# A transformer layer with top-1 expert routing: gate logits of four tiles at once, experts counted last in a step, half of the tiles stored turned

## The chip, the cores and the metric

The kernel runs on one core of a Trainium2 chip. The core has TensorE (PE, matrix products and transposes into PSUM), VectorE (DVE), ScalarE (ACT), GpSimd (POOL, here small powers, one addition per tile and indirect DMAs), and SyncE (SP), which here only issues DMAs. Each engine works through its own list in order, and semaphores tie the lists together. The metric is the device time of one execution in microseconds; lower is better.

## The reference, cut to what matters

```python
x = x + layernorm(attention(layernorm(x)))        # 2048 tokens of 512; local windows and 64 global queries per head
h = layernorm(x)                                  # 2048 x 512, the input of the gate and the experts
probs = softmax(h @ Wg); eidx = argmax(probs)     # 8 experts, one per token
pos   = running count of the token's expert, over all tokens in order
keep  = pos < 256                                 # each expert takes its first 256 tokens
xd[eidx * 256 + pos] = h                          # dispatch
oe    = (silu(xd @ W1) * (xd @ W3)) @ W2          # per expert, 512 -> 704 -> 512
shared = (silu(h @ sw1) * (h @ sw3)) @ sw2        # for every token
x = x + layernorm(gate * keep * oe[eidx * 256 + pos] + shared)
```

Products are made in about single precision: each operand is split into a rounded part and a rest (`fp32r`), and three products are added (`product3`). The change concerns `h @ Wg`, the running count, and how the second half of `h` is stored for the shared expert.

## The kernel before, in words

Tokens stand in 16 tiles of 128. The kernel has an attention part (until about 410 us), whose last steps already normalise tiles 0 to 3, and then twelve passes of the feed-forward network, held in the list `passes`: passes 0 and 1 are the shared expert on tiles 0 to 3 and 4 to 7, passes 2 to 9 are experts 0 to 7 with 256 rows each, passes 10 and 11 are the shared expert on tiles 8 to 15. A pass has `up` (six blocks m of 128 hidden units, each 24 products for m under 5 and 12 for m = 5, then `step(m)`), and `down` (pairs of output tiles, six blocks each, with `between` after each block). Products of passes 0, 1, 10 and 11 have 512 moving columns, those of the experts' `up` 256.

Beside passes 0 and 1 runs a software pipeline over the tiles, `work()`, one tick n per call: tick 7 ahead of pass 0, ticks 8 to 12 in `step(0)` to `step(4)` of pass 0, ticks 13 to 15 in `between` of its `down`, ticks 16 to 21 in `step(0)` to `step(5)` of pass 1. Tick n does, in this order, `h_logits(n-5)`, `h_turn(n-4)`, `h_h2(n-3)`, `h_mean2(n-2)`, `h_x1(n-1)`, `h_mean(n)`:

- `h_mean`, `h_x1`, `h_mean2` and `h_h2` normalise, add the residual, and write the normalised tile h2 (DVE statistics of L281 and L282, a power on POOL L284, ACT for the tile itself); `h_h2` also stores tiles 8 to 15 in `scr_h2` for passes 10 and 11.
- `h_turn` transposes h2 on PE (four transposes a tile) and copies it out: tiles 0 to 7 as two parts in XT (ACT the first, DVE the rest), the input of passes 0 and 1; tiles 8 to 15 whole in XL, only for the gate.
- `h_logits` multiplies the turned tile with the gate's weights. For tiles 0 to 7 the tile is the stationary operand and the 16 columns of `wghl` (two parts of 8 experts) move: eight products a tile. For tiles 8 to 15 it is four single-precision products, each two entries of the trace.
- After every fourth tile `route_count` finds the expert of each token and adds up counts on DVE (LG, OHB, CUM, CUMB). One tick later `route_place` takes OHB and CUMB as operands of sixteen tiny products on PE (eight times two), makes the row numbers FSI from them on DVE, and POOL scatters the four tiles into `scr_xd`. For the last four tiles it also does the softmax's sum.

Counts of group g run at ticks 8, 12, 16 and 20, right behind the logits of the group's last tile and ahead of the rest of the tick; `route_place` runs at ticks 9, 13, 17 and 21. DVE does in every `step(m)` the product and the rest of block m (SIL, HH), a rest of W2 (W2L), rests of W1 and W3 (W13L), and then the tick.

`prepare` loads the rows of a coming pass and turns them with `turned`, four transposes a tile. Rows for the experts come from `scr_xd`, and their first load waits for the last scatters: it is issued in the `down` of pass 1, and its tiles are turned in `between` at block 4 of the second pair. At the end of pass 1, `next_13` splits seven blocks of the next expert's W1 and W3 on ACT and DVE ahead of `down`, two of them ahead of tick 21 and five behind it.

PSUM banks: UP (four banks, in turn) for `up` and `route_place`, DN for `down`, TPC for transposes, MSC for logits.

Of the kernel before, what the change touches and what calls it, by code (L numbers as in the profile page):

```python
# [5 lines left out]
ALU = mybir.AluOpType  # L6
# [7 lines left out]
P = 128  # L14
# [6 lines left out]
E = 8  # L21
# [84 lines left out]
def sandwich(nc, x, wq, bq, wk, bk, wv, bv, wg, w1, w3, w2, s1, s3, s2, out):  # L106
# [16 lines left out]
    with ExitStack() as top:  # L123
# [56 lines left out]
        wghl = sb(top, "wghl", [P, 4, 2, E], F32R)  # L180
        wt8 = sb(top, "wt8", [P, E])
# [259 lines left out]
        with ExitStack() as st:  # L441
# [165 lines left out]
            def proj_group(g4):  # L607
# [39 lines left out]
                for n in range(2):  # L647
                    for c in range(4):
# [31 lines left out]
                        if n == 1 and c == 3 and g4 == 0:  # L680
                            m_wg.extend(split(wghl[:, :, 0, :], wghl[:, :, 1, :], wgs[:, :, :], "dve", [m_bias]))
                            stores.append(dma("sp", zs, lambda g: g.dma_start(
# [246 lines left out]
        def h_h2(t):  # L929
# [13 lines left out]
            if t >= 8:  # L943
                r0 = (t - 8) * P
                m = dma("sp", h2s[t % 2], lambda g: g.dma_start(h2d[r0:r0 + P, :], dst),
                        [m_h] + h2_marks[-2:-1])
                h2_marks.append(m)
                h2free[t % 8].append(m)

        def h_turn(t):  # L950
# [12 lines left out]
            else:  # L963
# [7 lines left out]
                TPC.busy[ti] += d["s"]  # L971
            h2free[t % 8].append(m_t)
# [311 lines left out]
        with ExitStack() as st:  # L1284
# [109 lines left out]
            scat = []  # L1394
            def h_logits(t):

                g4, j = divmod(t, 4)
                d = hs[t]
                if j == 0:
                    route["mi"], route["mb"], route["mfree"] = MSC.take()  # L1400
                mb, dst = route["mb"], d["dst"]
                if g4 < 2:
                    col = d["col"]
                    for k in range(4):
                        for l in range(2):
                            m_l = mm(mb[:, j * 16:(j + 1) * 16].rearrange("p (l e) -> p l e", l=2),
                                     dst[l][:, k, col:col + P], wghl[:, k, :, :], k == 0 and l == 0,
                                     k == 3 and l == 1, d["s"] + m_wg + route["mfree"], mark=(k == 3 and l == 1))
                    XT.busy[xt[g4]["i"]].append(m_l)
                else:  # L1410
                    for k in range(4):
                        m_l = mm(mb[:, j * 16:j * 16 + E], dst[:, k, :], wgs[:, k, :], k == 0, k == 3,
                                 d["s"] + m_wg + route["mfree"], mark=(k == 3))
                    XL.busy[d["li"]].append(m_l)
                route["m_l"] = m_l

            def route_count(g4):
# [3 lines left out]
                if g4 < 2:  # L1421
# [298 lines left out]
```

How the kernel before makes its waits and increments, by code:

```python
    def emit(self, e, eng):  # L90
        reached = {}
        for after, fn, inc in self.q[e]:
            need = {}
            for m in after:
                if m is not None and m.count > need.get(id(m.sem), (0, None))[0]:
                    need[id(m.sem)] = (m.count, m.sem)
            for key, (count, s) in need.items():
                if count > reached.get(key, 0):
                    eng.wait_ge(s, count)
                    reached[key] = count
            ins = fn(eng)
            if inc is not None:
                ins.then_inc(inc[0], inc[1])
```

## Time and profile before

| | us |
|---|---|
| median of 3 runs | 833.17 |
| lowest, highest | 830.14, 836.89 |
| profiled execution, its own time | 837.23 |
| its span | 835.5 |
| busy: PE, DVE, ACT, POOL | 783.1, 563.4, 423.3, 146.2 |
| mean granted clock of TensorE | 0.982 of full |

The profile is of one execution. Its times are from the first instruction of the span. The duration of a matmul in the trace contains its run through the array; what it takes in a row of matmuls is the distance between starts.

### The profile page before, as it was taken

What the parts mean: (1) busy time and instruction counts of PE and PEld (TensorE: products, weight loads), DVE (VectorE), ACT (ScalarE), POOL (GpSimd) and SP (SyncE); (2) the same over time, 40 slices, a digit from 0 to 9 for tenths busy, and PEclk for the clock granted to TensorE, in tenths of its full rate; (3) what the DMA queues carried; (4) which work ended last, traced back from release to release, by engine and by line L of the source; (5) the groups of instructions that cost most, each with busy time, mean ns of one, the idle gap of its engine ahead of it and who ended that gap; (6) DMA issues with size and microseconds to landing.
All of it is one profiled execution on the core that took longest, in us unless ns stands there. A gap on an engine that the chain in (4) does not pass through costs nothing.

```text
span 835.5 us, 13875 instructions
## 1 busy us (share of the span) xinstructions
PE 783.1 (94%) x5060; PEld 656.0 (79%) x5060; DVE 563.4 (67%) x1196; ACT 423.3 (51%) x839; POOL 146.2 (18%) x227
## 2 busy tenths in 40 slices
PE   4989999989999999999999999999999999999994
PEld 3768878767777777777778887899999999987883
DVE  4654699457888656777578656267766667848666
ACT  3455353525565666676545345466656666723120
POOL 2300010420110211333234631000000000013122
PEclk9989999999999999999999999999999999999998
DMA  6589554974767678873238831656877776546444
GB/s 211 190 248 344 185 175 157 293 205 130 205 161 202 171 201 234 237 214 105 78 102 286 322 127 58 195 175 205 252 215 239 235 223 212 176 164 184 169 152 138
DMA packets 117492, 162.39 MB, mean 194 GB/s; under 512 B 17364, under 2 KB 65236, under 8 KB 117424
## 3 DMA queue, kind: packets, MB, share of 16 engines
q1 hardware_dynamic: 113840, 153.54, 60.5%
q0 software_dynamic: 3584, 7.97, 3.2%
q8 instruction: 40, 0.66, 0.3%
q14 instruction: 28, 0.23, 0.1%
HBM read 107.24 MB, written 55.05 MB: 194 GB/s over the span
## 4 chain that ended last, share of the span: by engine, by line
PE 70%; DVE 15%; issue 5%; ACT 5%; DMA 3%; POOL 1%; POOLq 0%; DVEq 0%
PE bank L163 46%; PE wide L163 18%; PE wide L167 3%; PE bank L167 2%; DVE MX L160 2%; DVE SG L160 1%; ACT PTG L145 1%; ACT PT L157 1%; DMA QSe<-MR 1%; DVE GC L153 1%; DVE STC L281 1%; DMA XX<-scr_xd 1%; DVE TI L747 1%; DVE SIL L149 1%; DVE hl L149 1%
## 5 line engine op out<-in xcount | busy, mean ns | idle before, releaser
L163 PE MATMUL wide<-W2H,HH 128*128 128x512 f32 x308 | 101.9, 397 | 0.5 <-ACT OUTR L145 0.5
L160 DVE TENSOR_REDUCE MX<-wide 128x1 f32<-128x192 f32 (+1 forms) x128 | 77.6, 647 | 25.7 <-PE wide L163 20.2
L157 ACT ACTIVATE PT<-bank 128x512 f32<-128x512 f32 x128 | 73.4, 593 | 29.9 <-PE bank L163 27.7
L157 ACT ACTIVATE SIL<-bank 128x256 f32<-128x256 f32 (+1 forms) x72 | 32.6, 453 | 99.3 <-PE bank L163 99.0
L149 DVE TENSOR_TENSOR SIL<-bank,SIL 128x256 f32<-128x256 f32 (+1 forms) x72 | 36.9, 512 | 65.0 <-ACT SIL L157 64.4
L163 PE MATMUL bank<-XT,W13H 128*128 128x256 f32 (+1 forms) x336 | 76.6, 322 | 0.0
L145 ACT ACTIVATE HH<-SIL 128x256 fp32r<-128x256 f32 (+1 forms) x72 | 35.2, 489 | 67.2 <-DVE SIL L149 67.2
L163 PEld LDWEIGHTS wide<-W2H,HH 128*128 128x128 f32 x308 | 58.6, 190 | 13.2 <-ACT OUTR L145 1.3
L149 DVE TENSOR_TENSOR HH<-SIL,HH 128x256 fp32r<-128x256 f32 (+1 forms) x72 | 37.0, 514 | 45.5 <-ACT HH L145 35.0
L163 PE MATMUL wide<-W2L,HH 128*128 128x512 f32 x168 | 66.4, 395 | 0.8 <-DVE W2L L149 0.8
L163 PEld LDWEIGHTS bank<-XT,W13H 128*128 128x128 f32 x336 | 55.0, 188 | 4.7
L163 PE MATMUL bank<-WQL,W13H 128*128 128x256 f32 (+1 forms) x168 | 55.4, 330 | 0.0
L163 PE MATMUL bank<-WKL,W13H 128*128 128x256 f32 (+1 forms) x168 | 54.4, 324 | 0.0
L163 PE MATMUL bank<-WQL,W13L 128*128 128x256 f32 (+1 forms) x168 | 54.1, 322 | 0.0
L284 POOL TENSOR_TENSOR STC<-STC,mhalf 128x1 f32<-128x1 f32 x48 | 29.0, 604 | 140.5 <-DVE STC L153 135.9
L163 PE MATMUL bank<-XT,W13L 128*128 128x256 f32 (+1 forms) x168 | 53.6, 319 | 0.0
L163 PE MATMUL bank<-WVH,HT 128*128 128x512 f32 x128 | 41.9, 415 | 6.3 <-DVE HT L149 4.7
L163 PE MATMUL bank<-HT,WQH 128*128 128x512 f32 x128 | 42.4, 413 | 3.6 <-DVE HT L149 3.6
L149 DVE TENSOR_TENSOR W13L<-R,W13H 128x512 fp32r<-128x512 f32 x70 | 44.1, 688 | 1.7 <-ACT W13H L145 1.7
L1517 POOL DMA_INDIRECT H2A<-scr_oe,FG x8 | 8.0, 995 | 210.6 <-issue 210.6
L163 PE MATMUL bank<-XT,WQH 128*128 128x256 f32 (+1 forms) x192 | 43.0, 319 | 0.0
L149 DVE TENSOR_TENSOR W2L<-R,W2H 128x512 fp32r<-128x512 f32 x60 | 41.2, 687 | 1.5 <-issue 0.2
(256 smaller groups left out, 2019.0 us busy)
## 6 DMA issues: line engine op xcount, KB each, us to landing
R<-in_L_ffn_W_dram SPq DMA_DIRECT2D x48, 512.0 KB, 5.3
scr_q<-hl SPq DMA_DIRECT2D x16, 512.0 KB, 4.1
scr_k<-hl SPq DMA_DIRECT2D x16, 512.0 KB, 4.2
R<-in_L_ffn_sw_dram SPq DMA_DIRECT2D x12, 512.0 KB, 5.5
QSe<-scr_q SPq DMA_DIRECT2D x36, 128.0 KB, 3.9
KSe<-scr_k SPq DMA_DIRECT2D x36, 128.0 KB
scr_v<-vt SPq DMA_DIRECT2D x16, 272.0 KB, 2.2
R<-_attn_hidden_states_dram SPq DMA_DIRECT2D x16, 256.0 KB, 4.3
```

What stands on the lines that cost most here:

```text
L145: return do(e, lambda g: g.activation(dst, src, ACT.Copy), after)
L149: return do(e, lambda g: g.tensor_tensor(dst, a, b, op), after)
L153: return do(e, lambda g: g.tensor_scalar(dst, a, s1_, None, op0), after)
L157: return do("act", lambda g: g.activation(dst, src, fn, **kw), after)
L160: return do("dve", lambda g: g.tensor_reduce(dst, src, AXX, op), after)
L163: return do("pe", lambda g: g.matmul(ps, a, b, start=start, stop=stop, skip_group_check=True), after, mark=mark)
L167: return do("pe", lambda g: g.transpose(ps, a, idn), after, mark=mark)
L281: a = do("dve", lambda g: g.bn_stats(st[:, 8:14], src), after)
L284: return do("pool", lambda g: g.tensor_tensor(st[:, 2:3], st[:, 3:4], mhalf[:, :], ALU.pow), [a, m_half])
L747: m = do("dve", lambda g: g.max_index(i8, v8, N_[:, :]), prev)
L1517: mg = dma("pool", ga_slots[i], lambda e: e.indirect_dma_start(out=gb, out_offset=None, in_=oed, in_offset=bass.IndirectOffsetOnAxis(ap=FG ...
```

## The change

Gate. For tiles 0 to 3 and 4 to 7 `logits_group` makes the logits of four tiles in eight products: the 16 columns of `wghl` are stationary and 512 token columns of XT move, the result is 16 x 512. ACT copies it out to a buffer of XL, and one call later `logits_fold` turns it back with four single-precision products against `fold`, a 16 x 8 matrix of two identities, which also adds the two parts. `h_logits` remains for tiles 8 to 15. ACT's copy and one addition at the head of `route_count` become one DVE copy.

Order. In ticks 8, 16 and 20 `route_count` runs after everything else of the tick. The count of tiles 4 to 7 moves from tick 12 to `step(5)` of pass 0. `route_place` stays at ticks 9, 13 and 17, and that of the last group moves from `step(5)` of pass 1 to `between` behind the first block of its `down`, which is behind the seven splits of `next_13`.

Storage. Tiles 8 to 15 are stored from XL, turned, one tick later than before; passes 10 and 11 load them and split them from SBUF directly, without transposes.

```diff
--- before.py
+++ after.py
@@ -178,6 +178,7 @@
         onesb = sb(top, "onesb", [P, P], BF16)
         wgs = sb(top, "wgs", [P, 4, E])
         wghl = sb(top, "wghl", [P, 4, 2, E], F32R)
+        fold = sb(top, "fold", [2 * E, E])
         wt8 = sb(top, "wt8", [P, E])
         e256 = sb(top, "e256", [P, E])
         mhalf = sb(top, "mhalf", [P, 1])
@@ -679,6 +680,7 @@
                                 split_w(1, c)
                         if n == 1 and c == 3 and g4 == 0:
                             m_wg.extend(split(wghl[:, :, 0, :], wghl[:, :, 1, :], wgs[:, :, :], "dve", [m_bias]))
+                            m_wg.append(tt(fold[:, :], ident[0:2 * E, 0:E], ident[0:2 * E, E:2 * E], ALU.add, [m_id]))
                             stores.append(dma("sp", zs, lambda g: g.dma_start(
                                 xdd.rearrange("(i p) d -> p i d", p=P),
                                 zt[:, :].unsqueeze(1).broadcast_to([P, 16, D])), [k0]))
@@ -940,13 +942,6 @@
             XX.busy[xi].append(m_h)
             STC.busy[d["si"]].append(m_h)
             d["m_h"] = m_h
-            if t >= 8:
-                r0 = (t - 8) * P
-                m = dma("sp", h2s[t % 2], lambda g: g.dma_start(h2d[r0:r0 + P, :], dst),
-                        [m_h] + h2_marks[-2:-1])
-                h2_marks.append(m)
-                h2free[t % 8].append(m)
-
         def h_turn(t):
 
             g4, j = divmod(t, 4)
@@ -969,6 +964,11 @@
                 d["s"] = [copy("act", d["dst"][:, :, :], tb[:, :].rearrange("p (k t) -> p k t", k=4),
                                [m_t] + fr)]
                 TPC.busy[ti] += d["s"]
+                r0 = (t - 8) * P
+                m = dma("sp", h2s[t % 2], lambda g: g.dma_start(
+                    h2d[r0:r0 + P, :], d["dst"][:, :, :].rearrange("p k t -> p (k t)")), d["s"] + h2_marks[-2:-1])
+                h2_marks.append(m)
+                XL.busy[d["li"]].append(m)
             h2free[t % 8].append(m_t)
 
         with ExitStack() as st:
@@ -1392,37 +1392,47 @@
             route = dict(cum=m_cum)
             scat_slots = [slot() for _ in range(4)]
             scat = []
+            def logits_group(g4):
+
+                ui, ps, fr = UP.take()
+                li, lt, lf = XL.take()
+                x_ = xt[g4]
+                for l in range(2):
+                    for k in range(4):
+                        m_l = mm(ps[0:2 * E, :], wghl[:, k, :, :].rearrange("p l e -> p (l e)"),
+                                 x_["b"][l][:, k, :], k + l == 0, k + l == 4, x_["ready"] + m_wg + fr, mark=(k == 3 and l == 1))
+                XT.busy[x_["i"]].append(m_l)
+                m_c = copy("act", lt[0:2 * E, :, :].rearrange("p k t -> p (k t)"), ps[0:2 * E, :], [m_l] + lf)
+                UP.busy[ui].append(m_c)
+                route["lt"] = (li, lt, m_c)
+
+            def logits_fold():
+
+                li, lt, m_c = route["lt"]
+                route["mi"], route["mb"], fr = MSC.take()
+                for j in range(4):
+                    m_l = mm(route["mb"][:, j * 16:j * 16 + E], lt[0:2 * E, j, :], fold[:, :], True, True,
+                             [m_c] + m_wg + fr, mark=(j == 3))
+                XL.busy[li].append(m_l)
+                route["m_l"] = m_l
+
             def h_logits(t):
 
-                g4, j = divmod(t, 4)
+                j = t % 4
                 d = hs[t]
                 if j == 0:
                     route["mi"], route["mb"], route["mfree"] = MSC.take()
-                mb, dst = route["mb"], d["dst"]
-                if g4 < 2:
-                    col = d["col"]
-                    for k in range(4):
-                        for l in range(2):
-                            m_l = mm(mb[:, j * 16:(j + 1) * 16].rearrange("p (l e) -> p l e", l=2),
-                                     dst[l][:, k, col:col + P], wghl[:, k, :, :], k == 0 and l == 0,
-                                     k == 3 and l == 1, d["s"] + m_wg + route["mfree"], mark=(k == 3 and l == 1))
-                    XT.busy[xt[g4]["i"]].append(m_l)
-                else:
-                    for k in range(4):
-                        m_l = mm(mb[:, j * 16:j * 16 + E], dst[:, k, :], wgs[:, k, :], k == 0, k == 3,
-                                 d["s"] + m_wg + route["mfree"], mark=(k == 3))
-                    XL.busy[d["li"]].append(m_l)
+                for k in range(4):
+                    m_l = mm(route["mb"][:, j * 16:j * 16 + E], d["dst"][:, k, :], wgs[:, k, :], k == 0, k == 3,
+                             d["s"] + m_wg + route["mfree"], mark=(k == 3))
+                XL.busy[d["li"]].append(m_l)
                 route["m_l"] = m_l
 
             def route_count(g4):
 
                 mb, m_l, m_cum = route["mb"], route["m_l"], route["cum"]
                 lg = mb[:, 0:64].rearrange("p (j l e) -> p j l e", j=4, l=2)
-                if g4 < 2:
-                    a = copy("act", LG[:, 0, :, :], lg[:, :, 1, :], [m_l, m_cum])
-                    a = tt(LG[:, 1, :, :], lg[:, :, 0, :], LG[:, 0, :, :], ALU.add, [a])
-                else:
-                    a = copy("dve", LG[:, 1, :, :], lg[:, :, 0, :], [m_l, m_cum])
+                a = copy("dve", LG[:, 1, :, :], lg[:, :, 0, :], [m_l, m_cum])
                 L = LG[:, 1, :, :]
 
                 def bc(v):
@@ -1494,8 +1504,14 @@
                 d_ = xt.get(q)
                 if 0 <= n - 2 < rows:
                     xi, xb, m_ = d_["rows"][n - 2]
-                    m_t, s = turned(xb, d_["b"], (n - 2) * P, [m_], d_["free"], TPC)
-                    XX.busy[xi].append(m_t)
+                    c = (n - 2) * P
+                    if job < 9:
+                        m_t, s = turned(xb, d_["b"], c, [m_], d_["free"], TPC)
+                        XX.busy[xi].append(m_t)
+                    else:
+                        s = split(d_["b"][0][:, :, c:c + P], d_["b"][1][:, :, c:c + P],
+                                  xb[:, :].rearrange("p (k t) -> p k t", k=4), "act", [m_] + d_["free"])
+                        XX.busy[xi] += s
                     d_["ready"] += s
                 if n < rows:
                     xi, xb, xf_ = XX.take()
@@ -1559,15 +1575,18 @@
                 n = tick[0]
                 tick[0] += 1
                 if n == 7:
-                    h_logits(0)
-                    h_logits(1)
+                    logits_group(0)
+                if n == 8:
+                    logits_fold()
+                if n == 12:
+                    logits_group(1)
                 for back, fn in ((5, h_logits), (4, h_turn), (3, h_h2), (2, h_mean2), (1, h_x1), (0, h_mean)):
                     t = n - back
-                    if 4 <= t < 16 or 0 <= t < 4 and fn is h_logits:
+                    if (8 if fn is h_logits else 4) <= t < 16:
                         fn(t)
-                        if fn is h_logits and t % 4 == 3:
-                            route_count(t // 4)
-                if n % 4 == 1 and 9 <= n <= 21:
+                if n in (8, 16, 20):
+                    route_count((n - 8) // 4)
+                if n in (9, 13, 17):
                     route_place(n // 4 - 2)
 
 
@@ -1612,7 +1631,10 @@
                         else:
                             for g3 in range(3):
                                 load_13(1, g3)
-                    if q == 1 or q == 0 and m < 5:
+                    if q == 0 and m == 5:
+                        logits_fold()
+                        route_count(1)
+                    if m < 5 and q < 2:
                         work()
                     if job == 9:
                         t0 = 4 * (g - 2)
@@ -1647,6 +1669,8 @@
                     def between(t0, m):
                         if q == 0 and (t0, m) in ((0, 2), (2, 0), (2, 4)):
                             work()
+                        if q == 1 and (t0, m) == (0, 0):
+                            route_place(3)
                         if q == 1 and (t0, m) == (2, 4):
                             prepare(2, 2)
                             prepare(2, 3)
```

## Rows read from the trace of the kernel before

**Rows 1.** The page's engine row, whole span: busy time, its share, count of instructions.

```profile
PE 783.1 (94%) x5060; PEld 656.0 (79%) x5060; DVE 563.4 (67%) x1196; ACT 423.3 (51%) x839; POOL 146.2 (18%) x227
```

**Rows 2.** Waits of PE from 408 to 835: us in total, times, longest.

```profile
PE bank L163 <- DVE CUMB L146: 0.7, 1, 0.7
...
PE wide L163 <- DVE W2L L149: 0.8, 1, 0.8
```

**Rows 3.** Timeline of PE: start us, us, instruction; in brackets idle before, releaser.

```profile
410.11 0.26 PE L163 MATMUL wide<-wghl,WQL 128*128 128x16 f32 x1
...
412.79 0.75 PE L163 MATMUL bank<-WQL,WQH 128*128 128x512 f32 x1
...
428.17 1.03 PE L163 MATMUL wide<-wghl,XT 128*128 128x16 f32 x8 [1.32 <-DVE STC L935]
```

**Rows 4.** Chain of waits: start us, us of the piece, engine, count.

```profile
412.94 7.16 PE bank L163 x24
...
475.51 5.45 PE bank L163 x24
...
542.39 0.44 PE wide L167 x4
```

**Rows 5.** Windows: stretch, length, busy of each engine, granted clock, DMA.

```profile
412.80:416.00 3.20, 3.20 (x10) 2.53 (x10) 1.25 (x4) 1.28 (x1) 1.04 (x1) 0.51 0.21 60
...
429.70:433.20 3.50, 3.50 (x18) 2.72 (x14) 2.66 (x7) 2.01 (x4) 2.01 (x3) 0.53 0.34 95
...
515.10:518.80 3.70, 3.70 (x11) 2.87 (x10) 3.25 (x13) 3.65 (x7) 0.00 (x0) 0.54 0.00 0
```

**Rows 6.** Timeline of DVE around the first count.

```profile
424.92 0.18 DVE L149 TENSOR_TENSOR LG<-wide,LG 128x32 f32<-128x32 f32 x1
...
427.34 0.68 DVE L149 TENSOR_TENSOR XT<-wide,XT 128x512 fp32r<-128x512 f32 x1
...
430.48 0.68 DVE L149 TENSOR_TENSOR SIL<-bank,SIL 128x512 f32<-128x512 f32 x1
```

**Rows 7.** Timelines of DVE and PE around the second count.

```profile
460.45 0.69 DVE L149 TENSOR_TENSOR SIL<-bank,SIL 64x512 f32<-64x512 f32 x1
...
462.63 0.69 DVE L149 TENSOR_TENSOR W2L<-R,W2H 128x512 fp32r<-128x512 f32 x1
...
454.86 0.40 PE L163 MATMUL wide<-W2H,HH 128*128 128x512 f32 x1
...
460.23 0.17 PE L163 MATMUL bank<-OHB,trib 128*128 128x8 bf16 x1
```

**Rows 8.** Timelines of PE, DVE, POOL and SP at the end of pass 1.

```profile
513.02 0.18 PE L163 MATMUL bank<-OHB,trib 128*128 128x8 bf16 x1 [0.73 <-DVE OHB L146]
...
517.39 0.19 DVE L149 TENSOR_TENSOR LG<-bank,LG 128x32 f32<-128x32 f32 x1
...
519.35 3.16 DVE L149 TENSOR_TENSOR W13L<-R,W13H 128x512 fp32r<-128x512 f32 x5
...
519.37 0.98 POOL L1469 DMA_INDIRECT scr_xd<-H2B,FSI  x1 [19.58 <-DVE XS L1478]
...
526.77 0.80 SPq L1504 DMA_DIRECT2D XX<-scr_xd  x2
...
530.87 1.03 PE L167 MATMUL wide<-ident,XX 128*128 128x128 f32 x8
```

**Rows 9.** DMA issues from 500 to 600: count, KB each, median us to landing.

```profile
XX<-scr_xd SPq DMA_DIRECT2D x8, 256.0 KB, 3.4
```

**Rows 10.** A long wait of PE in the attention part, and the clock behind it.

```profile
184.72 0.79 PE L163 MATMUL bank<-QSe,KSe 97*128 97x256 f32 x2 [3.67 <-DMA QSe<-MR]
...
188.00:190.00 2.00, 2.00 (x15) 1.55 (x12) 0.00 (x0) 0.74 (x2) 0.00 (x0) 0.50 0.14 41
```

**Rows 11.** Timeline of DVE in pass 10.

```profile
747.35 0.69 DVE L149 TENSOR_TENSOR SIL<-bank,SIL 128x512 f32<-128x512 f32 x1 [1.01 <-ACT SIL L157]
...
769.20 0.68 DVE L149 TENSOR_TENSOR W2L<-R,W2H 128x512 fp32r<-128x512 f32 x1
```

## Prediction

> **What bounds the kernel now.** I read the page's engine row first: PE is busy 94% of the span, every other engine 67% or less [rows 1]. So time is won where PE does less or waits less, and lost where PE gets a new wait. Second, the waits of PE from 408 us on, the only part that the change touches in earnest: they are few and short, for CUMB (0.7 us) at the end of pass 1 and for W2L (0.8 us) in pass 10 [rows 2]. The timeline adds 1.3 us ahead of tick 9 [rows 3] and 0.7 us for OHB at the last count [rows 8]. Third, the granted clock: three stretches of 3.2 to 3.7 us at half of full (1.2 of 2.4 GHz), each behind a stretch in which PE idled or ran products of 16 or 8 columns [rows 5]. The price of one is in the chain: 24 products of 512 columns take 7.16 us across the first, 5.45 us at the full clock [rows 4], so 1.7 us. Fourth, DVE's timeline, because `route_place` on PE waits for DVE's counts, and DVE works through its list in order.
>
> **The change, part by part.** Against the profiled execution, in PE's time; plus is later.
>
> *Tick 7.* 24 products of 16 columns go: from 410.11 to 412.79, 2.7 us, 0.112 each [rows 3]. Eight of 512 columns come, at 5.45 / 24 = 0.227 each [rows 4]: 1.8 us. Gain 0.9. ACT's copy of 16 x 512 is off the path, since ACT has nothing until block 0 ends, some 7 us later [rows 4].
>
> *Tick 8.* Tile 3's eight products (0.9 us) go, the fold comes: four single-precision products, eight entries. No row has a stationary operand of 16 rows and 128 columns; the bounds are 0 and 8 x 0.112 = 0.9 us [rows 3]. I take 0.8, since the nearest rows also load 128 columns for a few moving ones. Change: 0. The Trainium skill (TensorE: Matmul & The Clock Gate, LDWEIGHTS) says that a load of weights takes its time from the columns and not from the rows; by that rule the fold costs the upper bound; no row here shows it. If rows counted, two folds would save 1.4 us more.
>
> *First count and tick 9.* This is where I differ from the obvious reading. Before, DVE did the count from 424.92 to 427.34 (2.42 us), then XT's rest and the statistics, and took up block 1's SIL at 430.48 [rows 6]. PE came to tick 9 at 428.17 - 1.32 = 426.85 and waited for XT [rows 3]. Now XT and the statistics come first, and the count ends where the statistics ended, 430.48, less the 0.9 of tick 7: 429.6. Tick 9 has no logits any more, so PE arrives at 426.85 - 0.9 + 0.44 for the transposes [rows 4] = 426.4, finds `route_place` next in its list, and waits 3.2 us for CUMB. Block 2 starts at 429.9 with the tiny products; before, at 429.7 [rows 5]. All of the gain is gone: running sum +0.2.
>
> *Ticks 10 to 12 and step 5.* Three tiles' logits go (2.7 us), eight wide products (1.8) and a fold (0.8) come: -0.1. Tile 7's transposes may wait half a microsecond for a DVE that has not become faster. Running sum +0.1 to +0.6.
>
> *Second count.* Its DVE work moves from ahead of block 5's SIL (460.45) to behind W2L (462.63) [rows 7]. Relieved of 2.42 and 0.9 us, W2L starts at 459.3 and ends at 459.9; the count ends at 462.4. `route_place` stays at tick 13, which PE reached at 460.23 [rows 7] and now reaches at about 460.5. It waits 1.5 to 2 us, queued behind it the second half of the first pair of `down`. Running sum +2.2.
>
> *Third count.* Behind the statistics it ends some 2 us later than before, still ahead of PE: 0.
>
> *Last count.* PE no longer waits 0.73 and 0.7 us [rows 2, 8], since one block of `down` runs first, and the slow stretch of 515 to 519 should go: 3.1 us. But on DVE the placing now stands behind five splits of W13L that it preceded, 3.1 us [rows 8]. With it move FSI, the four scatters (first at 519.37), and the loads from `scr_xd` that SP issues when the last scatter has landed, 526.77 [rows 8]. A load takes 3.4 us [rows 9]: 526.77 + 3.4 = 530.2, and PE turned the tiles at 530.87 [rows 8]. The slack was 0.7 us at most; I take 0.4. Late by 3.1, the turn moves by +2.7, and the 3.1 us that PE won are spent waiting there, some 5.8 us in one piece. The bounds are +3.1 (no slack) and, if the loads did not bind, -3.1.
>
> *Clock.* Stretch one (412.8) follows the light products of tick 7; wide ones stand there now, and I count it as gone: -1.7, bounds 0 and -1.7. Stretch two stays, since PE idles more ahead of it. A new one comes behind the second count's wait together with tick 13's light products: +1.7, bounds 0 and +1.7. The wait at the end of pass 1 is longer; the nearest row is the 3.67 us wait at 184.72, behind which the clock was still at half up to 190 [rows 10]. Half of those 5.3 us is a loss of 2.6, half of a short stretch as in rows 5 is 1.7; I take 2.0.
>
> *Transposes of tiles 8 to 15.* Four tiles in pass 9, four in pass 10, 0.44 us each [rows 4]. Pass 9 gives 1.8 us. In pass 10 DVE is the pace: idle until 747.35, and from there its list runs to W2L at 769.20 [rows 11], for which PE then waits 0.8 us [rows 2]. The splits remain, so PE arrives earlier and waits longer: 0, with -1.8 as the other end.
>
> *Stores.* A store of h2 now waits for XL's copy and stands ahead of the x1 store and the loads of its tick on SP. Those loads are used two ticks (about 14 us) later, which covers a delay of 1 to 2 us: 0. If that cover were gone, DVE's statistics, and with them the counts, would be late by as much. GpSimd's x1 addition is earlier, as the statistics are.
>
> Sum: +2.2 (both counts, with all of the gate's gain in it) - 1.7 + 1.7 (clock of ticks 7 and 13) + 2.7 + 2.0 (end of pass 1) - 1.8 = +5.1 us, 837.2 to 842.3. The profiled execution is 4.1 above the median of 833.2, so 838.3 for a median.
>
> **Rivals.** *The counts are in time (faster).* The three waits and three slow stretches vanish. PE sheds 64 x 0.112 = 7.2, takes 16 x 0.227 = 3.6 and 1.6 for folds: -2.0. Waits 1.3 + 1.4, stretches 5.1, pass 9 1.8: together -11.6, a median of 821.6. For it: this is what the edits add up to on PE, and the waits are real [rows 2, 3, 8]. Against it: DVE's count would have to end at 426.4 and 460.5, and I find 429.6 and 462.4. It decides at 3 us of DVE's list. Chance 0.15.
>
> *The loads from `scr_xd` do not bind.* If DVE reaches the placing as early as before, for instance because splits no longer wait for ACT's table load, pass 1 ends 3.1 us earlier instead of 2.7 later and without the slow stretch: +2.2 - 3.1 - 1.8 = -2.7, 830.5. Against it: the five splits alone take 3.1 us. Chance 0.15.
>
> *Slower: the clock.* Long waits bring long slow stretches, as in rows 10. Stretch one stays (0 in place of -1.7), the one behind tick 9 lasts 5.8 us instead of 3.5 (+1.1), the new one comes (+1.7), and the one at the end of pass 1 costs 2.9: 2.2 + 1.1 + 1.7 + 2.7 + 2.9 - 1.8 = +8.8, 842.0. It decides on how long the clock stays low behind waits of 3.2 and 5.8 us. For it, rows 10; against it, that row's matmuls have few rows to move and may be too light. Chance 0.20.
>
> *The storing does not do what it says.* If ACT or DVE set the pace of pass 9 too, as they do in pass 10, its 1.8 us stay: 840.1, inside my forecast's own range.
>
> **How the numbers follow.** The forecast, with the fold, slack and clock at their bounds, spans 834 to 841.5 and has 0.50. About 1%, 8 us, is what a measurement of this kernel can tell from no change. Faster by over 1% is the first rival, 0.15; slower by over 1% the third, 0.20; the rest, 0.65, is within 1%. The range for 8 in 10 takes the second rival and most of the third, with their scatter of some 3 us: 827 to 844.
>
> **What would show it.** PE waits for CUMB 3 us ahead of block 2 and 1.5 to 2 us in tick 13. The clock stays full at 413 and drops near 464 and near 530. PE waits 5 to 6 us for XX from `scr_xd` at the end of pass 1, and the first scatter of the last group starts 3 us later against block 5 of pass 1. Pass 9 is 1.8 us shorter, pass 10 unchanged, with a longer wait for W2L. I would be wrong if CUMB were ready at tick 9, or if XX were there before PE.

## The result, and the profile after

After: 838.2 us median (833.3 to 840.7), before in the same comparison 833.8 (830.1 to 838.6): a ratio of 1.0044 (95% interval 1.0029 to 1.0059), so 2.4 to 4.9 us slower, inside 1%. (This ratio is the estimate of the whole comparison; the two medians alone, divided, give 1.0053, or 4.5 us.) The forecast was 838.3. The profiled execution of after took 836.7 us against 837.2 of before: it ran 2.88 us faster up to tick 7, in a part that the change doesn't touch (before had lost 3.67 us to a load there, [rows 10], and after only 1.54). So all places below are counted from the start of tick 7, 410.11 before and 407.23 after; 2.88 added back to an end of 816.60 against 816.95 makes the change +2.5 us in this pair of profiles. The profiled execution of after is one of the better ones: its mean granted clock was 0.983, that of 12 of the 17 executions 0.979, which over 835 us is some 3.3 us less of full clock (an estimate from these two numbers); where they lose it no trace shows.

Page of after, the engine row, and PE's waits from 408 to 835 (us in total, times, longest); they answer to [rows 1, 2]:

```profile
PE 780.0 (93%) x4996; PEld 649.2 (78%) x4996; DVE 564.2 (68%) x1197; ACT 423.7 (51%) x839; POOL 145.0 (17%) x227
```

```profile
PE wide L167 <- DMA XX<-scr_xd: 3.0, 1, 3.0
PE wide L163 <- DVE W2L L149: 2.5, 1, 2.5
PE bank L163 <- DVE OHB L146: 2.0, 1, 2.0
PE bank L163 <- DVE CUMB L146: 1.0, 2, 0.7
PE wide L163 <- ACT W13H L145: 0.7, 1, 0.7
PE wide L163 <- ACT OUTR L145: 0.7, 2, 0.5
PE bank L163 <- DVE STC L937: 0.5, 1, 0.5
PE wide L167 <- ACT GC L157: 0.2, 1, 0.2
```

PE is busy 3.1 us less, and all of it, and more, comes back as waits: three of 2.0 to 3.0 us where before had none over 1.4 [rows 2, 3, 8]. PE's timeline in ticks 7 to 9:

```profile
407.23 1.11 PE L163 MATMUL bank<-WQL,wghl 128*16 128x512 f32 x4
...
409.11 0.40 PE L163 MATMUL bank<-WQL,WQH 128*128 128x512 f32 x1
...
414.68 1.05 PE L163 MATMUL wide<-fold,XL 16*128 16x8 f32 x8
415.67 0.65 PE L167 MATMUL wide<-ident,H2B 128*128 128x128 f32 x4
...
424.27 0.18 PE L163 MATMUL bank<-OHB,trib 128*128 128x8 bf16 x1 [2.02 <-DVE OHB L146]
425.16 0.19 PE L163 MATMUL bank<-CUMB,onesb 128*128 128x8 bf16 x1 [0.71 <-DVE CUMB L146]
```

The group product takes 1.9 us and the fold 1.0 (distances between starts). DVE's timeline says why the placing waits: the count (LG to CUMB, 422.42 to 425.01) now stands behind XT's rest (419.28) and the statistics (to 422.42), and SIL behind it, as [rows 6] had SIL behind the statistics:

```profile
419.28 0.68 DVE L149 TENSOR_TENSOR XT<-wide,XT 128x512 fp32r<-128x512 f32 x1
...
422.42 0.18 DVE L146 COPY LG<-wide 128x32 f32<-128x32 f32 x1
...
424.92 0.18 DVE L146 CAST CUMB<-CUM 128x32 bf16<-128x32 f32 x1
425.01 0.68 DVE L149 TENSOR_TENSOR SIL<-bank,SIL 128x512 f32<-128x512 f32 x1
```

The end of pass 1, DVE, POOL, SP and PE, answers to [rows 8]. All seven splits now stand ahead of the placing (LG, 518.69); scatters and loads follow; PE waits at the end of the chain:

```profile
514.35 4.31 DVE L149 TENSOR_TENSOR W13L<-R,W13H 128x512 fp32r<-128x512 f32 x7
518.69 0.19 DVE L149 TENSOR_TENSOR LG<-bank,LG 128x32 f32<-128x32 f32 x1
```

```profile
520.67 0.97 POOL L1479 DMA_INDIRECT scr_xd<-H2B,FSI  x1 [22.49 <-DVE XS L1488]
...
526.86 0.80 SPq L1520 DMA_DIRECT2D XX<-scr_xd  x2
...
529.58 1.76 PE L167 MATMUL wide<-ident,XX 128*128 128x128 f32 x8 [3.00 <-DMA XX<-scr_xd]
```

The clock, windows of all engines (the granted clock is the number ahead of the last two), answers to [rows 5]:

```profile
412.80:416.00 3.20, 3.20 (x20) 2.59 (x19) 0.58 (x1) 0.60 (x1) 2.89 (x5) 1.00 0.04 10
424.00:428.00 4.00, 3.02 (x14) 2.44 (x15) 3.07 (x10) 2.27 (x5) 0.00 (x0) 0.55 0.62 198
428.00:432.00 4.00, 4.00 (x12) 3.12 (x11) 3.86 (x11) 1.22 (x2) 1.29 (x2) 0.59 0.00 0
512.00:516.00 4.00, 3.80 (x23) 3.19 (x24) 3.17 (x6) 3.08 (x6) 0.00 (x0) 1.00 0.00 0
528.00:532.00 4.00, 2.42 (x11) 2.00 (x12) 0.69 (x1) 1.19 (x2) 0.00 (x0) 0.78 0.36 121
532.00:536.00 4.00, 4.00 (x26) 3.50 (x25) 0.69 (x1) 2.48 (x3) 0.00 (x0) 0.79 0.56 167
768.00:772.00 4.00, 3.95 (x12) 3.11 (x13) 3.80 (x8) 0.00 (x0) 2.24 (x3) 0.65 0.80 212
```

The stretches at 412 and 515 are at the full clock now; the one behind tick 9 is longer; two are new, each behind a long wait: 3.00 us at 529.58, 2.52 at 768.05 in pass 10:

```profile
768.05 0.47 PE L163 MATMUL wide<-W2L,HH 128*128 128x512 f32 x1 [2.52 <-DVE W2L L149]
```

### The profile page after: what moved, and what is told of

Same layout as the page of the kernel before. It is cut to its first block and busy times, and to the rows that moved or that the text cites. A ratio compares the mean times of both kernels' runs of the same rounds, so it can differ in the third digit from the quotient of the medians.

```text
span 834.9 us, 13757 instructions
## 1 busy us (share of the span) xinstructions
PE 780.0 (93%) x4996; PEld 649.2 (78%) x4996; DVE 564.2 (68%) x1197; ACT 423.7 (51%) x839; POOL 145.0 (17%) x227
```

## The experiments

The theory: from tick 8 to the end of pass 0, at the end of pass 1 and in pass 10 DVE's list, worked through in order, says when PE can go on. What the change takes off PE there turns into waits, and what it moves down DVE's list is waited for in full. Rivals: the new work itself (fold, ACT's copies, stores queued on SP) costs the time; or the order alone does, and DVE has time to spare.

Two lengths are read off PE's timeline of each profile: from the start of tick 7 to the start of pass 2, and pass 10, from its first product to that of pass 11. Ratios are to the kernel before on the same chip.

| Kernel | ratio (95%) | tick 7 to pass 2 | pass 10 |
|---|---|---|---|
| before | 1 | 123.4 | 48.7 |
| after | 1.0044 (1.0029 to 1.0059) | 125.6 | 50.3 |
| placed_before_splits | 0.999 (0.9956 to 1.0023) | 121.9 | 50.3 |
| place_a_tick_later | 1.0035 (1.001 to 1.0061) | 127.5 | 50.2 |
| turn_in_pass_10 | 1.0016 (0.9987 to 1.0044) | 126.5 | 48.7 |
| stored_straight | 1.0043 (1.0017 to 1.0069) | 125.2 | 49.3 |
| splits_and_turn_10 | 0.9982 (0.9957 to 1.0007) | 121.9 | 48.8 |
| first_count_ahead | 0.9967 (0.995 to 0.9984) | 122.1 | 48.6 |
| pool_subtracts | 1.0083 (1.0059 to 1.0107) | 121.9 | 55.6 |
| gate_alone | 1.0011 (0.9991 to 1.0032) | 125.3 | 49.8 |
| w2_in_the_gap | 0.9966 (0.9946 to 0.9986) | 121.8 | 46.8 |
| before_w2_in_the_gap | 0.9969 (0.995 to 0.9988) | 119.4 | 47.7 |
| relieved_and_reordered | 0.9922 (0.9897 to 0.9948) | 118.8 | 47.2 |
| before_relieved_turned_store | 0.9963 (0.9941 to 0.9986) | 121.4 | 48.1 |

**The last placing ahead of the five splits (placed_before_splits).**

```diff
-                if last:
+                if last and q != 1:
                     for m in range(3, 6):
                         next_13(m)
...
                             route_place(3)
+                            for m_ in range(3, 6):
+                                next_13(m_)
```

> The changed kernel, with the five splits of W13 at the end of pass 1 put behind the last placing instead of ahead of it; nothing else moves. Theory (the placing behind five splits holds up scatters, loads and so PE): the first scatter of the last group starts some 3.1 us earlier against block 5 of pass 1, PE's wait of 3.0 us for XX shrinks to about 0.5, the slow stretch behind it (3.4 us at half clock, 1.7 us) goes, together 4.2 us less than the changed kernel, level with the kernel before (0.999 to 1.000 of it). Rival (the loads are late for another reason, or W13L becomes what pass 2 waits for): no gain over the changed kernel, PE's wait only changes its name.

PE's waits from 500 to 560, and DVE's timeline (placing, then the five splits):

```profile
PE bank L163 <- DVE WKL L149: 0.6, 1, 0.6
PE wide L163 <- ACT OUTR L145: 0.5, 1, 0.5
PE wide L167 <- DMA XX<-scr_xd: 0.4, 1, 0.4
PE bank L163 <- DVE CUMB L146: 0.2, 1, 0.2
```

```profile
517.50 0.19 DVE L149 TENSOR_TENSOR LG<-bank,LG 128x32 f32<-128x32 f32 x1
...
519.46 3.15 DVE L149 TENSOR_TENSOR W13L<-R,W13H 128x512 fp32r<-128x512 f32 x5
```

The wait falls from 3.00 to 0.41 us and the low clock behind it is gone; pass 2 starts 3.8 us earlier. Of these 3.8, 0.7 were there already when PE came to the turn (118.6 against 119.3 us after tick 7), because this profile has no low clock behind tick 9; that is scatter between executions and not the edit. The other 3.1 are the place of the placing on DVE's list: 2.6 us of wait, and 0.5 between the turn and pass 2, where the low clock is gone and PE now waits 0.6 us for WKL.

**Placing a tick later (place_a_tick_later).**

```diff
-                if n in (9, 13, 17):
+                if n in (10, 14, 18):
                     route_place(n // 4 - 2)
```

> The changed kernel, with the placing of the first three groups one tick later (ticks 10, 14 and 18 instead of 9, 13 and 17). Theory A (the waits for the counts and the slow stretch behind them are what they cost): PE's waits of 2.7 and 0.5 us and 3.4 us for the stretch go, 6.6 us less than the changed kernel, 0.996 of the kernel before. Theory B (DVE's list paces ticks 8 to 12 as soon as PE is faster, since a tile can be turned only when DVE's statistics are through): PE waits for h2 at the transposes of ticks 10 and 11 instead, and only 1 to 2 us are won.

PE's waits from 408 to 470:

```profile
PE wide L167 <- ACT H2B L157: 2.7, 1, 2.7
PE wide L167 <- ACT H2A L157: 2.5, 1, 2.5
PE bank L163 <- ACT PTG L145: 0.3, 1, 0.3
```

The waits for OHB and CUMB are gone, and PE waits as long for H2B ahead of block 3, because ACT can't form it before DVE's statistics are there: block 3 starts 24.0 us after tick 7, against 24.1 in placed_before_splits. The 2.5 us for H2A come from the edit itself. ACT's timeline shows what H2A waited for:

```profile
454.82 0.81 ACT L157 ACTIVATE H2A<-XX,STC 128x512 f32<-128x512 f32 x1 [4.92 <-DMA scr_xd<-H2A,FSI]
```

The first group's scatters, which read the H2A buffers, now start only at 447.75, and ACT can't write the next tile there before the scatter from it has landed; DVE's statistics had been ready since 451.1. So `down` of pass 0 starts 47.8 us after tick 7 (after: 45.1). That the order on PE is not the cause is shown up to block 3; behind it the new wait covers what the move might have won.

**Tiles 12 to 15 turned in pass 10 (turn_in_pass_10).** These four are stored straight and turned by PE, as before; 8 to 11 stay turned.

```diff
+            if t >= 12:
...
+                m = dma("sp", h2s[t % 2], lambda g: g.dma_start(h2d[r0:r0 + P, :], dst),
+                        [m_h] + h2_marks[-2:-1])
...
-                    if job < 9:
+                    if job < 9 or g == 3:
                         m_t, s = turned(xb, d_["b"], c, [m_], d_["free"], TPC)
```

> The changed kernel, with tiles 12 to 15 stored as before and turned by PE in pass 10 again; tiles 8 to 11 stay turned. Theory (DVE paces pass 10; PE's longer wait for W2L, 2.5 us, drops the clock, and that costs more than the transposes did): 1.8 us more PE work in pass 10, PE waits 0.8 us for W2L, no slow stretch in pass 10, the pass is 1.6 us shorter than in the changed kernel. Rival (transposes on PE cost what they take): the pass is 0 to 1.8 us longer.

PE's waits from 720 to 790 are 0.8 us for W2L and 0.8 for W13H, there is no low clock in the pass, and it takes 48.7 us again. So sixteen transposes fewer in pass 10 cost 1.6 us. W2L of block 5 starts 39.1 to 39.2 us behind the start of the pass with and without them (before 769.20 - 730.01, [rows 11]; after 767.22 - 728.07; here 772.45 - 733.32): PE, 1.75 us ahead, waits 1.75 us more, and behind the longer wait the clock is low for 1.6 us of loss. All fourteen profiles agree on that pass: a low stretch stands behind the waits of 2.46, 2.47, 2.52 and 5.60 us, and none in the ten profiles whose wait in `down` of pass 10 is 1.84 us or less.

**Tiles stored straight (stored_straight).** The storage undone for all eight (h2 stored straight in `h_h2` too), the gate's part kept.

```diff
-                    if job < 9:
+                    if True:
                         m_t, s = turned(xb, d_["b"], c, [m_], d_["free"], TPC)
```

> The changed kernel, with the storage of tiles 8 to 15 undone altogether; the gate and the order stay. Theory: pass 9 is 0.9 us longer, pass 10 1.6 us shorter, so 0.7 us less than the changed kernel: the storage brings nothing. Rival (eight tiles of 0.44 us are saved): 3.5 us more than the changed kernel.

Pass 9 takes 25.4 us, as before (after: 24.4); pass 10 takes 49.3: DVE waits 0.67 us there for gathered rows (H2A from `scr_oe`), for which it does not wait in turn_in_pass_10. The whole is where after is. The turned storage, 32 transposes less, is worth nothing as long as DVE paces pass 10: -0.9 in one pass, +1.0 to +1.6 in the other.

**Both repairs together (splits_and_turn_10).** Edits one and three.

> The first and the third experiment together: the five splits of W13L behind the last placing, and tiles 12 to 15 stored straight and turned by PE in pass 10. Theory (the two losses are independent and lie at the end of pass 1 and in pass 10): the wait for XX at the end of pass 1 below 0.6 us, the W2L wait of pass 10 below 1 us with no low clock in 700 to 820 us; 3.8 + 1.6 = 5.4 us less than the change, a ratio to the kernel before of 0.997 to 0.999. Rival (what is won at the end of pass 1 is waited for later, since DVE or ACT paces passes 2 to 9): passes 2 to 9 get longer by 2 to 4 us in sum, ratio 1.001 to 1.003.

XX wait 0.5, W2L wait 0.8, passes 2 to 9 195.0 us long against 195.2 after: in the profile nothing is waited for later, and the repairs add up. The intervals of the ratios are too wide to show the sum by themselves.

**The first count ahead (first_count_ahead).** On top of it, the count directly behind the fold.

```diff
                 if n == 8:
                     logits_fold()
+                    route_count(0)
```

> As the kernel beside it (splits behind the placing, tiles 12 to 15 straight), and the first group's count stands right behind the fold of tick 8, ahead of the tick's turning and statistics. Theory (tick 9 waits for DVE's list, in whatever order): DVE's sum does not change, so block 2 starts when XT and the statistics are done, 17.2 to 17.6 us after the start of tick 7 in place of 18.1: PE's wait is then for STC and not for CUMB; the gain is 0.5 to 0.9 us. Rival A (only the order cost the gain): PE waits less than 1 us ahead of block 2, which starts 16.2 us or less after tick 7. Rival B (the fold and ACT's copy are late, so that the count holds up XT): block 2 later than 18.1.

PE's waits from 408 to 470:

```profile
PE wide L167 <- ACT GC L157: 2.4, 1, 2.4
PE wide L167 <- ACT H2B L157: 2.0, 2, 1.6
PE wide L163 <- ACT OUTR L145: 0.2, 1, 0.2
```

Block 2 starts 16.8 us after tick 7, between the theory's 17.2 and rival A's 16.2; PE waits 1.55 us ahead of it, for H2B (not for STC, but H2B hangs on STC). What is won is waited for at tile 7's transposes: 2.35 us for GC, and PE is there 31.7 us after tick 7, against 31.9 in five kernels with the count at the tick's end. Two orders of the count, one arrival: that is what one expects if DVE's sum, and not its order, sets it. This is the first kernel whose interval lies below 1, though it can't be told from the one without the edit.

**POOL forms XT's rest in passes 9 and 10 (pool_subtracts).**

```diff
+                        a_ = copy("act", d_["b"][0][:, :, c:c + P], src_, [m_] + d_["free"])
+                        s = [a_, tt(d_["b"][1][:, :, c:c + P], src_, f(d_["b"][0][:, :, c:c + P]), ALU.subtract,
+                                    [m_, a_] + d_["free"], e="pool")]
```

> The splits of W13L behind the last placing, storage turned for tiles 8 to 15 as in the change, but in passes 9 and 10 POOL and not DVE forms the rest (XT's low part). Theory (DVE paces pass 10): about 4 x 0.6 us leave DVE's list, W2L is ready earlier, the wait for it is below 1.5 us and there is no slow stretch behind it: pass 10 takes 48.0 to 48.8 us in place of 50.3, and the whole is within 0.5 us of the kernel with straight tiles beside it. Rival (the loads of XX or ACT's part set the pace, or POOL is too slow and XT's rest comes late): pass 10 50 us or more, with PE waiting for XT at its start.

The theory of this run failed: PE waits 3.0 us for W2L in pass 9 and 5.6 in pass 10, which takes 55.6 us. POOL and DVE subtract side by side eight times, four in each pass; two of the four of pass 10:

```profile
747.92 1.31 POOL L149 TENSOR_TENSOR XT<-XX,XT 128x512 fp32r<-128x512 f32 x1 [1.17 <-issue]
...
769.65 1.27 POOL L149 TENSOR_TENSOR XT<-XX,XT 128x512 fp32r<-128x512 f32 x1
```

```profile
748.40 1.38 DVE L149 TENSOR_TENSOR W2L<-R,W2H 128x512 fp32r<-128x512 f32 x1 [0.32 <-ACT W2H L145]
...
769.16 2.33 DVE L149 TENSOR_TENSOR W2L<-R,W2H 128x512 fp32r<-128x512 f32 x1 [0.39 <-ACT W2H L145]
```

DVE's subtraction takes 0.69 us elsewhere; here it takes 1.30 to 2.33 us and ends 0.55 to 0.57 us behind POOL's recorded end, in all eight pairs. By these times it stood still while POOL subtracted. The Trainium skill (SBUF — State Buffer, Who interferes with whom) says that a DVE `tensor_tensor` with both inputs in SBUF and a GpSimd operation that reads SBUF exclude each other and the later one blocks fully; the trace agrees for W2L at 748.40; for the one at 769.16 the recorded starts show DVE ahead of POOL, and yet DVE ended behind it. Of DVE's 0.6 us a tile nothing is saved: W2L of block 5 starts 41.6 us behind the start of the pass, not 39.1, and then takes 1.6 us longer.

**The gate alone (gate_alone).** Storage, the three other counts and the last placing as before.

> The group logits and the folds alone: tiles stored and turned as in the kernel before, counts of the first, third and last group at the front of their ticks, last placing in tick 21 ahead of the splits. The second count stands at block 5 of pass 0 as in the change. Theory (the change's gate part is worth what its two slow ticks give back, and the rest of the loss is in the last placing and the storage): tick 8 starts 2.4 us earlier than before relative to tick 7, block 2 about 0.9 to 1.5 earlier, the end of pass 1 has before's waits (0.7 for OHB, 0.7 for CUMB) and slow stretch; 1 to 3 us less than the kernel before, a ratio of 0.997 to 0.999. Rival (DVE paces block 0 to the end of pass 0, so the gain is waited for): the start of down of pass 0 within 0.3 us of before and a ratio of 1.000 to 1.001.

Between the two: block 2 starts 2.8 us earlier than before, but `down` of pass 0 44.0 us after tick 7 (before 44.8), with 1.56, 0.47 and 2.35 us of waits for H2B and GC ahead of it. The 0.8 is lost again, and 1.8 more by the start of pass 1 (67.0 against 65.2): the second count stands at block 5 as in the change (0.5 us wait for CUMB, which the profile puts down to STC, DVE's next instruction), and the clock is 0.57 in 460 to 464. The ratio is that of no change.

**W2's split in the gap (w2_in_the_gap).** In the passes with 512 columns DVE waits about 0.8 us in nearly every block between SIL and HH, for ACT's half of HH. Here W2's split is issued into it, in passes 0 and 10.

```diff
+                    if gap:
+                        gap(m)
                     lo = HH[r, 1, m, 0:N] if m < 5 else HH[0:64, 0, 5, 0:N]
...
-                    if first:
+                    if first and job not in (0, 9):
                         split_2(job, m, "act")
...
+                                 (lambda m: split_2(job, m, "act")) if first and job in (0, 9) else None)
```

> The change with one reordering: in pass 0 and in pass 10 the split of W2 (ACT's W2H, DVE's W2L) is issued between DVE's SIL product and the two parts of HH, not behind HH, so that it falls into the 0.77 us in which DVE waits for ACT's HH. Theory (DVE's list is what paces ticks 8 to 12 and pass 10, and PE waits because of it): each block of DVE's list gets up to 0.7 us shorter; block 2 starts 17.3 to 17.6 us after tick 7 in place of 18.1, down of pass 0 at 41.5 to 43.5 in place of 44.1 to 45.1; in pass 10 W2L of block 5 is ready 2 us or more earlier, PE's wait for it is below 0.8 in place of 2.52, no low clock there, and the pass takes 46.5 to 48 us in place of 50.3. Together 4 to 7 us less than the change, a ratio to the kernel before of 0.996 to 1.000. Rival (PE or the loads pace these stretches and the waits only mark the order): both stretches within 0.5 us of before the edit, ratio 1.003 to 1.005.

DVE's timeline in pass 10, and its waits from 740 to 763:

```profile
746.47 0.68 DVE L149 TENSOR_TENSOR SIL<-bank,SIL 128x512 f32<-128x512 f32 x1
747.07 0.68 DVE L149 TENSOR_TENSOR W2L<-R,W2H 128x512 fp32r<-128x512 f32 x1
747.92 0.69 DVE L149 TENSOR_TENSOR HH<-SIL,HH 128x512 fp32r<-128x512 f32 x1 [0.17 <-ACT HH L145]
```

```profile
DVE SIL L149 <- ACT SIL L157: 1.6, 1, 1.6
DVE CX L1554 <- DMA H2A<-scr_oe,FG: 1.2, 2, 0.6
```

The idle before HH is 0.17, and not a product was taken away. Block 2 starts 17.5 us after tick 7, `down` of pass 0 42.3, W2L of block 5 starts 36.5 us behind the start of pass 10 (after: 39.1), PE waits 0.6 (for HH) there, no low clock, 46.8 us: each of the theory's numbers. The ratio to before is 0.9966, about 0.8% below that of after (1.0044). DVE now waits for gathered rows instead, 0.6 us twice: perhaps the next bound.

**The same for the kernel before (before_w2_in_the_gap).**

> The kernel before with the same reordering alone. Theory: it has less to wait for (1.32 us for STC ahead of tick 9, 0.77 us for W2L in pass 10), so it wins 1.5 to 3 us: ratio 0.996 to 0.998; and so with DVE relieved the change is worth more against this kernel than it was against the one before: after with the reordering over before with it 0.998 to 1.001 where the change alone gave 1.0044. Rival (the change's loss has nothing to do with DVE's pace): that quotient stays at 1.004.

The ratio is 0.9969, and there is no wait of PE in 700 to 790. The change costs 0.9966 / 0.9969 = 0.9997 when DVE is relieved (0.997 to 1.0025, both errors combined), 1.0044 when it isn't. Here some cancelling is seen: the change still loses 2.4 us up to pass 2 (2.9 us wait for XX) and now wins 0.9 each in passes 9 and 10. The profiles don't bear out the quotient place by place: passes 2 to 8 took 1.3 us longer with the change (a wait of 1.2 us for XX against 0.3), and from tick 7 to the end it is 1.9 us behind.

**All orders repaired (relieved_and_reordered).** Gap, last placing ahead of the splits, first count ahead, tiles stored turned.

> The change with the reordering of W2's split, the last placing ahead of the five splits of W13L, and the first count ahead of the rest of its tick; tiles 8 to 15 stored turned, as in the change. Theory (the three losses are separate and are all in DVE's order): no wait of PE above 1.5 us behind tick 7, XX wait below 0.6 us, pass 10 46.5 to 48 us: 8 to 11 us less than the change, ratio 0.991 to 0.995. Rival (the losses overlap, PE's work is the bound once two are gone): 0.996 or more.

The median is 827.1 us against 832.9 of before, a ratio of 0.9922 (0.9897 to 0.9948), the best; it beats both kernels. Its profile has no clock below full from 400 us to its last product's tail. One number was missed: a wait of 1.69 us for GC where none above 1.5 was expected.

**Before, relieved, with the turned storage (before_relieved_turned_store).** Without the gate's part.

> The kernel before with W2's split in the gap and with the change's turned storage of tiles 8 to 15, and nothing of its gate or of its order of counts. Theory A (with DVE relieved the transposes' 1.8 us come through, and the group logits are worth under 1 us because DVE, not PE, still sets ticks 8 to 11): pass 9 24.4 us, pass 10 46.8 to 47.2 us, pass 2 starts 119.4 us after tick 7 as it did with the reordering alone; ratio to the kernel before 0.994 to 0.996, within 0.002 of the kernel with everything. Theory B (the group logits carry the gain of the best kernel): ratio 0.996 or more, over 0.003 behind it.

Inconclusive, nearer to theory B: 0.9963, 0.0041 behind the best, with an error of 0.0034 on that difference and on another chip. Pass 9 took 24.4 us, as expected, pass 10 48.1 and not 47: DVE waited 1.9 and 0.6 us for gathered rows, H2A from `scr_oe`. Pass 2 started 121.4 us after tick 7 and not 119.4. Two low stretches, behind the logits of tick 7 and at the end of pass 1, are there in its profile and not in the best's. But this profile is of the slowest of its twelve executions (839.1 us, median 832.8), and before_w2_in_the_gap, with the same logits and the same placing, had the full clock at both places. So that the group logits keep such stretches away is not shown, and what they are worth stays open.

## Why the prediction was right, and where only by cancelling

The median came as forecast (838.3 against 838.2), and the change stays within 1%. The prediction's own markers, as running sums from tick 7 against before:

| Place | forecast | measured |
|---|---|---|
| start of tick 8 | -2.6 | -2.4 |
| start of block 2 | -1.5 | -1.5 |
| `down` of pass 0 | -1.6 to -1.1 | +0.3 |
| behind the second placing | +0.5 | +1.4 |
| start of pass 1 | +2.2 | +1.1 |
| start of pass 2 | +6.9 | +2.2 |
| start of pass 10 | +5.1 | +0.9 |
| start of pass 11, and the end | +5.1 | +2.5 |

- **Ticks 7 to 9: right** in mechanism and size. The group product and the fold took 2.9 us where 2.6 was put down; the clock stayed full at 412.8; PE waited 2.0 + 0.7 us at `route_place`, 3.2 forecast. The Trainium skill's rule (TensorE: Matmul & The Clock Gate, LDWEIGHTS) that a load is priced by columns bears on the fold's price: a 16 x 128 load took 187 ns in after's profile, a 128 x 128 one 188. The trace agrees. The fold took 1.0 us, a little over the prediction's upper bound of 0.9.
- **The clock behind tick 9: mis-sized.** "Stretch two stays", but it was longer: 0.55 and 0.59 over eight microseconds, 3.4 us lost where before lost some 1.7. Idle and clock don't go together firmly: with the same 2.0 + 0.7 us of waits, placed_before_splits had the full clock there, and four other kernels lost half as much as after.
- **Second count: mis-sized.** 1.5 to 2 us of wait forecast, 0.5 measured. With 2.88 added, DVE took up W2L at 458.3, not 459.3, the count ended at 461.6, not 462.4, and PE came at 461.1, not 460.5. The low clock behind tick 9 is not why the wait was short: in placed_before_splits, without it, both came 0.7 us earlier and the wait was 0.5 again. What was wrong is the 459.3 for DVE; why DVE was there sooner, no run singles out. The new low stretch (+1.7) did not come in after; gate_alone and turn_in_pass_10 had one there, some 52 us after tick 7.

DVE's timeline of after around it, W2L to CUMB:

```profile
455.45 0.69 DVE L149 TENSOR_TENSOR W2L<-R,W2H 128x512 fp32r<-128x512 f32 x1
456.17 0.19 DVE L146 COPY LG<-wide 128x32 f32<-128x32 f32 x1
...
458.51 0.18 DVE L146 CAST CUMB<-CUM 128x32 bf16<-128x32 f32 x1
```

- **Last count: the mechanism right, the size half.** Scatters moved by +3.1 (first at 520.67 - 407.23 = 113.4 against 109.3, less the 1.1 of pass 1's start). But from the first scatter to the loads it took 6.2 us, not the 7.4 of [rows 8], and the loads themselves were faster, as the two views below show. Before's second load landed at 530.97; after's second landed 0.6 us behind its first, so before's first landed at about 530.3 (an estimate), 3.6 us behind its issue against 2.7 after, and 0.5 us ahead of the turn: the forecast's slack of 0.4 was about right, its two times were not. 3.1 - 1.2 - 0.9 - 0.5 = +0.5 for the turn against +2.7; PE waited 3.0 and not 5.8, and the low clock (0.78 and 0.79) made the stretch from the turn to pass 2 longer by 1.3, of which 0.7 took the place of before's wait for WKL: +0.6 and not +2.0.

The DMA issues of 526 to 528, before and after (the median counts only landings that the trace has):

```profile
XX<-scr_xd SPq DMA_DIRECT2D x2, 256.0 KB, 3.8
```

```profile
XX<-scr_xd SPq DMA_DIRECT2D x2, 256.0 KB, 2.8
```

- **Pass 9: half.** 0.9 of 1.8 came; PE then waits 0.7 for ACT's W13H. Neither this wait nor its owner was in the forecast.
- **Pass 10: the step that failed.** It was put at "0, with -1.8 as the other end", because DVE paces. That is right, and the wait grew by just the 1.75 us that PE saved. What was missing is that a wait costs the clock too: +1.6, outside both ends. At the end of pass 1 the prediction had priced a longer wait that way.

In the pair of profiles the sum is +2.5, not +5.1: the end of pass 1 was priced 3.6 us too high and what precedes it 1.1, passes 9 and 10 2.5 too low, and 0.3 fell away between. By the ratio of the comparison it is 3.7 (2.4 to 4.9), by the two medians 4.5. For a profiled execution the same sum said 842.3, and it took 836.7. That the median agrees to a tenth of a microsecond is luck; the sign, and that the waits for CUMB and XX and the low clock at the end of pass 1 came where they were forecast, are not. The rival "slower: the clock" named the mechanism that pass 10 showed. The rival in which the loads from `scr_xd` do not bind was wrong as a forecast and is right as a repair: placed_before_splits is that kernel.

## What to carry to other kernels

In this kernel, and so worth a look in others: where an engine other than the busiest works its list in order and the busiest waits at its end, taking work off the busiest buys a wait, and with TensorE possibly a low clock: worse than nothing. First fill that engine's own gaps; here one call moved into such a gap won more than the whole change had lost. When a step is moved, count what already stands in its new place on every queue behind it, and ask of each step whose output goes to memory and back whether anything without a deadline stands in front.

## What the runs showed of the hardware

- A DVE subtraction with both inputs in SBUF stood still during a POOL subtraction that reads SBUF, and ended 0.55 us after it in eight pairs of eight (pool_subtracts; 0.69 us became 1.30 to 2.33). DVE's SIL product, which has one input in PSUM, kept its 0.68 us beside POOL's addition (after, 447.95).
- Eight products with the gate's 16 columns held took 0.23 us each, the same as with 128 columns held: the 512 columns that move set the time.
- A buffer that POOL scatters from is taken for long: in place_a_tick_later ACT could write H2A again 7.1 us after the first scatter's start, and the last scatter took 6.8 us to land.
- Behind waits of 2.5 and 3.0 us the clock was low for parts of the next 8 us (0.65 and 0.93; 0.78 and 0.79), while the same 2.35 us wait for GC was followed by 0.68 in 440 to 444 in first_count_ahead and by the full clock in gate_alone. What decides between them is open.
